# Reordered first loads, a direct load of LoRA B and interleaved quarters in the opening of an NF4 feed-forward kernel

## The reference

```python
# cond: a linear layer with a LoRA adapter chosen for each batch
base  = einsum('bsi,oi->bso', x, weight) + bias1
low   = einsum('bsi,bri->bsr', x, lora_a[adapter_id])
delta = einsum('bsr,bor->bso', low, lora_b[adapter_id])
c     = base + scale[adapter_id][:, None, None] * delta
# ffn: NF4 weight, 16 levels, one absmax per 64 codes
wq    = NF4[codes] * absmax
out   = x + (einsum('bsd,od->bso', c, wq) + bias2)
```

## Time and profile before

| | us |
|---|---|
| median of 3 runs | 2225.14 |
| lowest, highest | 2223.64, 2225.20 |
| the profiled execution | 2223.64 |
| its span in the trace | 2221.9 |
| start of job 2 in the trace | 110.55 |

### The profile page before, as it was taken

How to read it: one execution, slowest core, us unless ns; L and a number is a source line. 1 busy time by engine, 2 the same in 40 slices (tenths; PEclk the granted TensorE clock), 3 DMA queues, 4 the chain that set the end, 5 groups by cost and what they waited for, 6 DMA issues and landing times.

```text
span 2221.9 us, 31532 instructions
## 1 busy us (share of the span) xinstructions
PE 2166.7 (98%) x12104; PEld 1862.7 (84%) x12104; DVE 1789.5 (81%) x2655; ACT 1018.2 (46%) x1277; POOL 24.4 (1%) x33
## 2 busy tenths in 40 slices
PE   3799999999999999999999999999999999999999
PEld 3688778787878787899999988888988889888888
DVE  6899879868975574688887898888898887888887
ACT  6655555555554333444444434333444334443332
POOL 3100000000000000000000000000000000000000
PEclk7899999999999999999999999999999999999999
DMA  9587788887888897877777887787977778877775
GB/s 275 192 254 246 249 251 254 264 252 250 255 260 253 280 286 243 273 243 236 240 242 232 272 277 243 242 248 243 297 256 247 244 246 256 291 251 246 240 244 173
DMA packets 380948, 558.00 MB, mean 251 GB/s; under 512 B 23152, under 2 KB 234768, under 8 KB 380672
## 3 DMA queue, kind: packets, MB, share of 16 engines
q1 hardware_dynamic: 377712, 544.95, 77.3%
q0 software_dynamic: 3088, 11.03, 1.5%
HBM read 427.96 MB, written 128.99 MB: 251 GB/s over the span
## 4 chain that ended last, share of the span: by engine, by line
PE 95%; DMA 2%; ACT 1%; DVE 1%; issue 0%; SPq 0%; DVEq 0%; ACTq 0%
PE ps L1408 26%; PE ps L1242 15%; PE ps L1244 15%; PE ps L1243 15%; PE ps L1409 13%; PE ps L1412 4%; PE ps L1257 2%; PE ps L1411 2%; PE ps L1290 1%; DMA code_w<-in_L_ffn_codes_dram 1%; PE ps L1238 1%; DMA raw<-in_L_cond_weight_dram 0%; DMA xr<-xc_d 0%; ACT wq_nat_w L666 0%; ACT tile L685 0%
## 5 line engine op out<-in xcount | busy, mean ns | idle before, releaser
L1408 PE MATMUL ps<-comb,xs 128*128 128x512 f32 x2527 | 903.2, 395 | 0.0
L727 ACT CAST xs<-xr 128x1024 fp32r<-128x1024 f32 x427 | 449.7, 1054 | 623.3 <-DMA xr<-xc_d 622.7
L1409 PE MATMUL ps<-comb,xs 128*128 128x256 f32 x2527 | 707.8, 280 | 0.0
L1014 DVE TENSOR_TENSOR xs<-xr,xs 128x1024 fp32r<-128x1024 f32 x427 | 521.4, 1222 | 126.8 <-ACT xs L727 124.0
L1408 PEld LDWEIGHTS ps<-comb,xs 128*128 128x128 f32 x2527 | 474.3, 188 | 102.4
L1409 PEld LDWEIGHTS ps<-comb,xs 128*128 128x128 f32 x2527 | 475.4, 188 | 14.5
L1242 PE MATMUL ps<-wq,tile 128*128 128x512 f32 x1088 | 468.2, 430 | 3.9 <-DVE tile L948 3.9
L1244 PE MATMUL ps<-wq,tile 128*128 128x512 f32 x1088 | 427.4, 393 | 0.0
L1243 PE MATMUL ps<-wq,tile 128*128 128x512 f32 x1088 | 426.5, 392 | 0.0
L1242 PEld LDWEIGHTS ps<-wq,tile 128*128 128x128 f32 x1088 | 205.6, 189 | 71.5 <-DVE tile L948 3.7
L1244 PEld LDWEIGHTS ps<-wq,tile 128*128 128x128 f32 x1088 | 205.2, 189 | 45.1
(11 more groups left out here) (119 smaller groups left out, 2199.8 us busy)
## 6 DMA issues: line engine op xcount, KB each, us to landing
xr<-xc_d SPq DMA_DIRECT2D x427, 512.0 KB, 4.0
raw<-in_L_cond_weight_dram SPq DMA_DIRECT2D x128, 512.0 KB, 4.4
xc_d<-rq SPq DMA_DIRECT2D x26, 1792.0 KB, 7.5
res<-in_x_dram SPq DMA_DIRECT2D x64, 512.0 KB, 5.4
out_dram<-res SPq DMA_DIRECT2D x128, 256.0 KB, 4.5
wc_d<-cs SPq DMA_DIRECT2D x32, 896.0 KB, 4.7
comb_raw<-wc_d SPq DMA_DIRECT2D x28, 1024.0 KB, 7.7
x_nat<-in_x_dram SPq DMA_DIRECT2D x104, 256.0 KB, 3.9
```

Of the source, the lines that this page charges most:

```text
L727: nc.scalar.copy(xs[f][:, HI, :, :], xr[f][:, LO, :, :]).then_inc(s_xhi, 1)
L1014: tt(xs[f][:, LO, :, :], xr[f][:, LO, :, :], xs[f][:, HI, :, :].bitcast(F32), ALU.subtract).then_inc(s_xlo, 1)
L1408: nc.tensor.matmul(bank[:, :], x_hi, both, start=(k == 0), stop=False)
L1409: nc.tensor.matmul(bank[:, 0:HW], x_lo, high, start=False, stop=False)
```

## The change

It has four parts, and the whole diff follows. SP's first loads are put into another order: the second pair of codes goes directly behind the first, `absm` ahead of `ident`, and all groups 2 to 9 of x behind codes 4 and 5. POOL waits for codes 2 and 3 before it loads LoRA A, and for codes 4 and 5 before LoRA B. LoRA B no longer goes by `b_cols` for the first column group: 16 DMAs (one per adapter and half, 1024 runs of 64 bytes) write it into `raw[0]` and `raw[1]`. `b_cols` is filled later, one adapter after each of the tiles 3 to 10 has been multiplied, and `bias1` is loaded after the last early store, with a semaphore of its own. On TensorE the quarters of jobs 0 and 1 stand behind the piece of their step.

```diff
--- before.py
+++ after.py
@@ -269,6 +269,7 @@
 
         s_const = sem("const_loaded")
         s_small = sem("small_loaded")
+        s_b1 = sem("bias1_loaded")
         s_bcols = sem("b_cols_stored")
         s_code = [sem(f"codes_loaded{i}") for i in range(3)]
         s_code_w = [sem(f"wide_codes_loaded{i}") for i in range(3)]
@@ -372,6 +373,8 @@
                     sp.wait_ge(s_acc, g - 1)
                 s = g % S1
                 if s == 0:
+                    if h == 0 and g == S1:
+                        sp.wait_ge(s_bcols, 16 * NA)
                     src = b_cols.rearrange("(k p) c -> p k c", p=P)[:, h * HK:(h + 1) * HK, :]
                 else:
                     t = TILE_ORDER[s - 1]
@@ -475,15 +478,14 @@
 
             load_codes(0)
             load_codes(1)
-            sp.dma_start(ident[:, :], identity).then_inc(s_const, 16)
-            sp.dma_start(absm[:, :, :], absmax.rearrange("(t p b) -> p t b", p=P, b=NQ)).then_inc(s_const, 16)
-            load_early_groups(0, 2)
             load_codes(2)
             load_codes(3)
-            load_early_groups(2, 5)
+            sp.dma_start(absm[:, :, :], absmax.rearrange("(t p b) -> p t b", p=P, b=NQ)).then_inc(s_const, 16)
+            sp.dma_start(ident[:, :], identity).then_inc(s_const, 16)
+            load_early_groups(0, 2)
             load_codes(4)
             load_codes(5)
-            load_early_groups(5, SLOTS)
+            load_early_groups(2, SLOTS)
             load_codes(6)
             load_codes(7)
             load_early_groups(SLOTS, early_before(1) + SLOTS)
@@ -618,22 +620,27 @@
             pool.dma_start(ids_i[:, :], itok.partition_broadcast(P)).then_inc(s_small, 16)
             pool.dma_start(scale_c[:, :], bass.AP(scaling.tensor, scaling.offset, [[1, NA], [0, R], [1, 1]])
                            ).then_inc(s_small, 16)
-            pool.dma_start(b1_nat[:, :], bias1.rearrange("(t p) -> p t", p=P),
-                           allow_slow_non_contiguous=True).then_inc(s_small, 16)
+            pool.wait_ge(s_code_w[1], 32)
             pool.dma_start(a_nat[:, :], lora_a.rearrange("a r i -> (a r) i")).then_inc(s_a_nat, 16)
-            for a in range(NA):
-                pool.dma_start(b_cols[:, a * R:(a + 1) * R], lora_b[a]).then_inc(s_bcols, 16)
+            pool.wait_ge(s_code_w[2], 32)
+            for h in range(2):
+                for a in range(NA):
+                    pool.dma_start(raw[h][:, LO, :, a * R:(a + 1) * R],
+                                   lora_b[a, h * HK * P:(h + 1) * HK * P, :].rearrange("(k p) r -> p k r", p=P)
+                                   ).then_inc(s_b_ld[h], 16)
             store_early(0)
-            pool.wait_ge(s_bcols, 16 * NA)
-            for h in range(2):
-                pool.dma_start(raw[h][:, LO, :, :], b_cols.rearrange("(k p) c -> p k c", p=P)[:, h * HK:(h + 1) * HK, :]
-                               ).then_inc(s_b_ld[h], 16)
             for m in range(1, EARLY - 1):
                 store_early(m)
             pool.wait_ge(s_a_raw, 1)
             pool.dma_start(a_sel_d.rearrange("b p f -> p b f"),
                            a_raw[:, :, :, :, :].rearrange("p b h k r -> p b (h k r)")).then_inc(s_a_st, 16)
             store_early(EARLY - 1)
+            pool.dma_start(b1_nat[:, :], bias1.rearrange("(t p) -> p t", p=P),
+                           allow_slow_non_contiguous=True).then_inc(s_b1, 16)
+            for a in range(NA):
+                pool.wait_ge(s_acc, a + 4)
+                pool.dma_start(b_cols[:, a * R:(a + 1) * R], lora_b[a]).then_inc(s_bcols, 16)
+
 
         def evacs(g):
             return g - g // S1
@@ -681,7 +688,7 @@
                 if g:
                     act.wait_ge(s_ld[slot], 16 * ((g + 1) // 2))
                 else:
-                    act.wait_ge(s_b_ld[h], 16)
+                    act.wait_ge(s_b_ld[h], 16 * NA)
                 nc.scalar.copy(tile[slot][:, HI, :, :], raw[slot][:, LO, :, :]).then_inc(s_hi, 1)
 
             def evacuate(g):
@@ -967,7 +974,7 @@
                     k, h = divmod(i, 2)
                     src, col = wq[j % 2][:, k, h, :].bitcast(F32), b1_nat[:, k:k + 1]
                     if i == 0:
-                        dve.wait_ge(s_small, 80)
+                        dve.wait_ge(s_b1, 16)
                         dve.wait_ge(s_qhi, PIECES * (j + 1))
                         dve.wait_ge(s_qlo, PIECES * (j + 1))
                         if j == 0:
@@ -1123,7 +1130,7 @@
             for w in range(WIDES):
                 dequantise_wide(w)
                 if w == 1:
-                    dve.wait_ge(s_small, 80)
+                    dve.wait_ge(s_small, 64)
                     link(nc.vector.tensor_copy(ids_f[:, :], ids_i[:, :]))
                     link(ts(ids_w[:, :], ids_f[:, :], 0.0, float(NA), ALU.is_lt, ALU.mult))
                     link(tt(ids_w[:, :], ids_w[:, :], ids_f[:, :], ALU.add))
@@ -1337,20 +1344,22 @@
                     for t in range(QK):
                         transpose_x(i, t)
                 if step == 5:
-                    multiply_tile(0, range(HK))
+                    multiply_tile(0, quarter[0])
+                if step < WIDES:
+                    transpose_piece(2 * step)
+                    transpose_piece(2 * step + 1)
+                else:
+                    transpose_piece(step + WIDES)
+                if step == 2:
+                    select_a()
+                if step == 5:
+                    multiply_tile(0, quarter[1])
                 if step == 6:
                     multiply_tile(1, quarter[0])
                 if step == 7:
                     multiply_tile(1, quarter[1])
-                if step == 9:
+                if step == 8:
                     multiply_tile(0, quarter[2])
-                if step < WIDES:
-                    transpose_piece(2 * step)
-                    transpose_piece(2 * step + 1)
-                else:
-                    transpose_piece(step + WIDES)
-                if step == 2:
-                    select_a()
             multiply_tile(1, quarter[2])
             multiply_tile(0, quarter[3])
             multiply_tile(1, quarter[3])
```

More of the change, by code:

```diff
@@ L1339, in _ @@
                 if step == 5:
-                    multiply_tile(0, range(HK))
[L1341 to L1344, removed]
-                if step == 9:
-                    multiply_tile(0, quarter[2])
+                    multiply_tile(0, quarter[0])
                 if step < WIDES:
@@ L1353, in _ @@
                     select_a()
+                if step == 5:
+                    multiply_tile(0, quarter[1])
+                if step == 6:
+                    multiply_tile(1, quarter[0])
+                if step == 7:
+                    multiply_tile(1, quarter[1])
+                if step == 8:
+                    multiply_tile(0, quarter[2])
             multiply_tile(1, quarter[2])
```

## The result

| kernel | median of 20 runs | lowest to highest |
|---|---|---|
| before | 2225.88 us | 2223.64 to 2229.24 |
| changed | 2221.07 us | 2216.58 to 2227.99 |

Each kernel ran 20 times on the same chip. The ratio of changed to before is 0.998, with a 95% interval of 0.9973 to 0.9986: 4.5 us faster, 3.1 to 6.0 by the interval (the two medians lie 4.8 apart). The forecast was 2215.3, and its range ended at 2220.2, so the direction was right, the time lies 0.9 us outside the range, and about half of the gain is missing.

A forecast was written before the change was run, and what follows sets the result against it. TensorE, busy for 98% of the span, bounds the kernel, so only job 2's start could move: 110.55 to 99.6 us, less 1.2 for slow matmuls, -9.8 in all. From 2225.14 that gives 2215.3 us; range 2210 to 2220.2.

The forecast's parts named there:

- Codes first: Opening: second pair of codes arrives early, so VectorE's idle 8.24 us before its second wide step go in full.
- What the codes are taken from: Opening: nearly the same bytes must land in 10 us less; 0 to 4 us given back, taken as 0.
- LoRA B straight to its tile: POOL's sixteen loads in the opening: last issued by 29.6 to 39.9 us, in time for ScalarE and early stores, so hidden.
- rival C: Opening becomes DMA-bound, or LoRA B's loads hold up POOL's early stores: 2 to 5 us given back, 2218 to 2220.5; chance 0.15.
- the port rule: VectorE's two-port `tensor_scalar` blocks GpSimd's descriptor writes: could add some 3 us to LoRA B's sixteen issues.
- TensorE's order: Slim pieces in the opening: VectorE's waits of 3.1 + 1.8 us go, stage 27.02 to 22.1, piece 15 ready at 84.5.
- What is late next: End of opening: group 23 transposed at 85.8, tile 2 lets job 2 start at 99.6; 4.3 us idle, slow matmuls 1.2.
- bias1 and `b_cols` later: Jobs after the opening: the late bias load is free, the eight `b_cols` DMAs are taken as 0.
- rival E: Jobs 4 to 11: `b_cols` DMAs delay tiles and TensorE waits, up to 31 us lost, 2246; slower, chance 0.05.
- The base: From job 2 on: 2111.35 us, unchanged, from the profiled 2223.64 us execution; 1.5 us added for the median.

The follow-up runs named there:

- e3: Changed kernel with LoRA B's sixteen 64-byte-run loads replaced by two loads of as many weight bytes in 512-byte runs; 2216.39 us, ratio to before 0.9961.
- e1: Kernel before with only TensorE's new order of quarters; 2222.06 us, ratio to before 0.9988.
- e5: Changed kernel with the eight loads of LoRA B's second half held until codes 10 and 11 have landed; 2215.50 us, ratio to before 0.9957.
- e11: Changed kernel with LoRA B's second half and tile 1's loads both issued late, the moves of e5 and e6; 2216.16 us, ratio to before 0.9966.
- e6: Changed kernel with tile 1's loads (1 MB) moved from ahead of codes 10 and 11 to behind code 13; 2216.24 us, ratio to before 0.9960.
- e4: Changed kernel with the first half of tile 2 loaded ahead of the three x loads that wait for the last transpositions; 2219.65 us, ratio to before 0.9972.
- e9: Changed kernel without the eight DMAs that fill `b_cols`, the other column groups reading `weight` instead; 2221.61 us, ratio to before 0.9987.
- e8: Kernel before, unedited, run once more with a second profile; 2224.52 us.

## What failed in the prediction, and what held

**Codes first.** Right. The second wide step started at 13.80 (I had 13.3), so 7.7 of the 8.24 us were won there, and no wait took its place; `absm` and the first groups were there.

**What the codes are taken from** ("Bounds: 0 to 4 us given back ... I take 0"). This is the step that failed, together with the "hidden" of **LoRA B straight to its tile**. The term that I put at 0 was 4.0 us at the first slim piece, and 2.9 us of it were left at job 2. The first slim piece came at 66.4, not 62.4: 0.5 us of later start, 2.9 lost through late codes 10 and 11, and 0.6 in smaller pieces. It was rival C, by another road than I had named (and 0.6 us above its range). I had followed LoRA B to those who use it (ScalarE's copy of tile 0) and to what stands behind it on POOL (the early stores). Neither was late. The loss passed through the shared DMA engines to SP's queue, and there to codes that have nothing to do with LoRA B. I had read the earlier trace rows, a share of 0.80 over the 51 us of the stage, as room. In the fifteen microseconds from 20 to 35, in which LoRA B's runs were written, there was none (1.04 to 1.08). Of the port rule that I had weighed nothing was seen: fifteen issues took 13.67 us beside an almost always busy VectorE, 0.91 each, as much as the two of e3 (1.79 us together). The 1.04 of the earlier trace rows are for DMAs of twice as many runs, so they are no measure of it, and no run isolates the rule.

**TensorE's order.** Right in size. ScalarE's waits of 5.09 and 4.04 us are gone (the longest for a transposition is 2.82), VectorE's 3.1 and 1.8 have become 0.6 and 0.8. From the first slim piece to piece 15 (89.1) it took 22.7 us; I had 22.1.

**What is late next.** Right, and shifted by the late start. Group 23 was transposed at 88.9 (85.8 plus 3.1 of the 4.0), the chain to job 2 took 13.57 us (13.78), the idle time was 3.59 (4.3), and the slow matmuls cost 1.2 (1.2). The last is luck in part: after idle stretches of 2.23, 2.64, 2.91 and 3.35 us (e1, e5, e3, e11) no matmul was slow, and after 2.63 (e6) seven were. e4 shows what I had not: even without this wait, VectorE's tiles keep TensorE from gaining more than half of it.

**bias1 and `b_cols` later.** Taken as 0. Two waits of 0.8 us together are the most that the trace shows of it, and e9 bounds the eight loads at about 1 us; rival E's 31 us did not come.

**The base.** I took 2111.35 us behind job 2 from one execution. 2.2 us of it were luck of that execution, as e8 shows, and I had corrected it by only 1.5. (Its job 2 started 1.2 us later than e8's, which works the other way.) This does not touch the comparison of medians much, but it is why the traces' difference is -3.1 and the medians' is -4.8.

In sum, of the 9.8 us forecast for the traces, 2.9 were lost before job 2, 1.5 between it and the products, and 2.2 lie in the base; 3.2 are left, which is the difference of the two spans.

**Open.** What in a run decides over the waits at the start of the products, and why e6 has none of those in jobs 10 to 13. Where the last 0.7 us between job 2 and the products are lost. Why the changed kernel's runs scatter over 11.4 us, and those of before over 5.6. Whether SP's issues are held by a full queue or by writing descriptors was not separated: the runs show only that the stall follows throughput and the megabyte ahead.

## What to carry to other kernels

When a load is moved next to others, price what its short runs do to the shared throughput in the microseconds in which they are written, and then walk the other queues' lists: whoever issues next pays, not the one whose load it is. A mean DMA share over a stage says nothing about room in a part of it. In an opening, what is needed last should be issued last, since a megabyte ahead of its time costs nothing only as long as the queue runs fast. And take a second profile of the kernel before, if a few microseconds matter: one execution's stage lengths were off by half of the gain here.

## What was unexpected of the hardware

- DMAs with 64-byte runs lower what everyone gets: 228 and 203 GB/s at shares of 1.07 and 1.04, against 367 and 373 at 1.04 and 1.08 with 512-byte runs, the same bytes and 2 DMAs instead of 16 (e3). The 8 DMAs of `b_cols` in the kernel before stood behind 191 at 1.03.
- The issue itself then becomes long: two DMAs occupied SP for 8.40 us, 7.93 of them the first alone, against 1.89 before and 0.87 when no megabyte stood ahead (e6). A long issue does not need short runs: at the start of the changed kernel `ident`, a single DMA behind four of codes and `absm`, held SP for 4.93 us from 3.08, before POOL had issued LoRA A or B.
